# A conditioned feed-forward layer and a generated adapter: ternary weights made over two steps, the generator's base summed on GpSimd, and the low halves of the activations made later

## The chip, the core and the metric

The kernel runs on one core of one Trainium2 chip. Its engines are TensorE (PE, matmuls), VectorE (DVE), ScalarE (ACT), GpSimd (POOL) and SyncE (SP, which here only issues DMAs). The metric is the device time of one execution in microseconds (us), taken as the median of several executions.

## The reference, cut to what matters

There are 32 sequences of 256 rows with 256 columns. Layer 0 is a feed-forward layer with a scaled norm, a gate, and a product in which activations and weights are quantized; layer 1 is an adapter whose weight matrices are generated for each sequence from its condition vector.

```python
# layer 0
scale = cond @ norm_w.T + 1.0
ms = jnp.mean(x * x, axis=-1, keepdims=True)
h = x * (scale[:, None, :] * jax.lax.rsqrt(ms + EPS))
u = h @ up_w.T                       # (rows, 2048)
val, gate = jnp.split(u, 2, axis=-1)
h = val * jax.nn.gelu(gate, approximate=False)
y = act_quant(h) @ weight_quant(down_w).T    # ternary weights: -1, 0, 1 over a scale
x = y + x
# layer 1
dWd = ((h_lang @ Wdd.T + bdd) * DELTA_SCALE).reshape(B, BN, D)
dWu = ((h_lang @ Wdu.T + bdu) * DELTA_SCALE).reshape(B, D, BN)
down = jax.nn.relu(jnp.einsum('bld,bnd->bln', x, Wd + dWd) + bd)
up = jnp.einsum('bln,bdn->bld', down, Wu + dWu) + bu
return x + up
```

## The kernel before

The rows are cut into 64 tiles of 128 (two to a sequence), and every engine runs a loop over steps `s` = 0, 1, 2, ...; step `s` holds the feed-forward work of tile `s` and, beside it, work of other tiles at fixed lags. Each engine's instructions are written out in program order and run in that order; engines meet at semaphores. There is no scheduler.

A product in nearly full precision is made of three matmuls of 16-bit parts: high by high, high by low, low by high. So most operands are split: `xs_hi` and `xs_lo` (scaled activations, `scaled_high` on ACT, `scaled_low` on DVE), `up_hi` and `up_lo` (up weights), `wsplit` (generator weights; `high_part` on ACT, `low_part` partly on DVE, L578, and partly on POOL as four instructions, L364).

In step `s` TensorE does, in this order: `up(s, 0)` (12 matmuls of 512 columns into `u_val[0]` and `u_gate[0]`), `down(s - 3)` (8 matmuls), `up(s, 1)` (12 matmuls), and then either `generate(s - 2)` (48 small matmuls, in steps 2 to 17), or the adapter's `middle` and `output`. `up(s, c)` overwrites the banks that tile `s - 1` left, so it waits until `gate(s - 1, c)` on DVE (L642, signalled as `hid_done`) has read them. `generate(q)` waits for both low parts of chunk `q`; its second half also waits for `evacuate(q - 1, 0)` on DVE (L588, signalled as `gen_done`), because the generator has three banks. `gelu(s, c)` on ACT (L471) reads `u_gate[c]` and needs the norm factor `rms` of the sequence, which POOL makes in `rsqrt(b)`: eleven small instructions in a row, L375 to L386.

`ternary()` on DVE makes the ternary down weights once, in step 1: a scale (L604, L607) and three passes over 2048 columns (L609, L612, L615). `base_sum()` on DVE adds the generator's bias to the static adapter weights, once, in step 2 (L597, L600). `scaled_low(b)` stands in step `2b - 1`, ahead of the residual (L716) and of the two evacuations of that step; TensorE asks for it in step `2b`:

```python
if s % TPB == 0:
    pe.wait_ge(xs_done, s // TPB + 1)
up(s, 0)
```

Before its first real work TensorE runs matmuls on a tile of ones, whose result nobody reads (`idle(IDLE_FIRST)`, `idle(IDLE_SECOND)`, L798).

SP's queue issues every large load in program order: activations (`load_x`), up and down weights, generator chunks (`load_chunk`, 1 MB each), and the transposes of the quantized tiles.

Of the kernel before, what the change touches and what calls it, by code (L numbers as in the profile page):

```python
# [16 lines left out]
ALU = mybir.AluOpType  # L17
# [4 lines left out]
B, S, D = 32, 256, 256  # L22
# [3 lines left out]
TPB = S // P  # L26
# [42 lines left out]


IDLE_FIRST = 8
IDLE_SECOND = 12


LAST_T = NT - 1
# [49 lines left out]
def build(nc, xT, xn, condT, norm_wT, up_wT, down_wT, WdT, bd, WuT, bu, WddT, bddT, WduT, bduT, out):  # L125
    with ExitStack() as ctx:
# [146 lines left out]
        def _(sp):  # L273
# [49 lines left out]
                sp.dma_start(bias_raw[:, i, :], b).then_inc(ld_small, 16)  # L323
            sp.dma_start(bd_col[:], bd).then_inc(ld_small, 16)
            sp.dma_start(bu_row[:], bu.to_broadcast([P, D])).then_inc(ld_small, 16)
            load_chunk(1)
            for s in range(END):
                if s <= NT:
                    for t in split_tiles(s - 1):
                        transpose_x1(t)  # L330
                if 0 <= s - 1 < NT:
                    transpose_q(s - 1)
                if s >= NT:
                    for t in split_tiles(s):
                        transpose_x1(t)
                for b in sequences(s, -2):
                    if b < LAST_B:
                        store(b)
                    else:
                        store_last()  # L340
                if s % TPB == 0 and s // TPB + 2 < B:
                    load_x(s // TPB + 2)
                for q in chunk(s, -2):
                    if q >= 2:
                        load_chunk(q)
# [6 lines left out]
        def _(pool):  # L352
# [50 lines left out]
            def output_bias(b):  # L403
# [4 lines left out]
                for i in range(TPB):  # L408
                    nc.gpsimd.tensor_tensor(out_s[:, b % OUT_SLOTS, i], x1[:, (b * TPB + i) % X1_SLOTS], bu_row[:], ALU.add  # L409
                                            ).then_inc(outb_done, 1)  # L410

            def middle_low(b):
                pool.wait_ge(relu_done, b * 2 + 2)
                nc.gpsimd.tensor_tensor(mid_lo[:], mid[:], mid_hi[:], ALU.subtract).then_inc(mid_done, 1)  # L414

            rsqrt(0)
            for s in range(END):
                for b in sequences(s, -1):
                    if b < LAST_B:
                        middle_low(b)  # L420
                if 0 <= s - 2 < NT:
                    dequantization(s - 2)
                for b in sequences(s, 0):
                    output_bias(b)
                if s == 1:
                    rsqrt(1)
                for q in chunk(s, 0):
                    low_part(q)
                for b in scales(s):
                    if b > 1:  # L430
                        rsqrt(b)
                for b in sequences(s, 2):
                    adapter_low(b)
# [123 lines left out]
        def _(dve):  # L557
# [24 lines left out]
            def evacuate(q, n):  # L582
                w = q // NGC
                at = (q % NGC * 2 + n) * 2 * BCH
                if q == 0:
                    dve.wait_ge(base_ready, 2)
                dve.wait_ge(gen_full, 2 * q + n + 1)
                nc.vector.scalar_tensor_tensor(  # L588
                    out=adapt[:, w, :, at:at + 2 * BCH].rearrange("p b m -> p m b"),
                    in0=gen_ps[(2 * q + n) % 3][:].rearrange("p (m b) -> p m b", b=B),  # L590
                    scalar=DELTA_SCALE * A_SCALE / (W_SCALE * C_SCALE),
                    in1=base[:, w, at:at + 2 * BCH].unsqueeze(2).to_broadcast([P, 2 * BCH, B]),
                    op0=ALU.mult, op1=ALU.add).then_inc(gen_done, 1)

            def base_sum():
                dve.wait_ge(ld_small, 16 * N_SMALL)
                nc.vector.scalar_tensor_tensor(out=base[:], in0=bias_raw[:], scalar=DELTA_SCALE, in1=base[:],  # L597
                                               op0=ALU.mult, op1=ALU.add).then_inc(base_ready, 1)
                dve.wait_ge(base_ready, 1)
                nc.vector.tensor_scalar(base[:], base[:], A_SCALE, None, ALU.mult).then_inc(base_ready, 1)  # L600

            def ternary():
                dve.wait_ge(absum_full, 1)
                nc.vector.tensor_scalar(wsum[:, 1:2], sum_ps, 1.0 / (D * FF), QUANT_EPS, ALU.mult, ALU.max  # L604
                                        ).then_inc(tern_ready, 1)
                dve.wait_ge(tern_ready, 1)
                nc.vector.reciprocal(wsum[:, 2:3], wsum[:, 1:2]).then_inc(tern_ready, 1)  # L607
                dve.wait_ge(tern_ready, 2)
                nc.vector.tensor_scalar(raw_down, raw_down, wsum[:, 2:3], ROUND, ALU.mult, ALU.add  # L609
                                        ).then_inc(tern_ready, 1)  # L610
                dve.wait_ge(tern_ready, 3)
                nc.vector.tensor_scalar(raw_down, raw_down, ROUND + 1.0, ROUND - 1.0, ALU.min, ALU.max  # L612
                                        ).then_inc(tern_ready, 1)
                dve.wait_ge(tern_ready, 4)
                nc.vector.tensor_scalar(tern[:].rearrange("p j d -> p (j d)"), raw_down, ROUND, None,  # L615
                                        ALU.subtract).then_inc(tern_ready, 1)
# [127 lines left out]
            for n in range(NC * KD):  # L744
# [3 lines left out]
                                               in1=up_part(up_hi, c, k), op0=ALU.mult, op1=ALU.subtract  # L748
                                               ).then_inc(up_ready, 1)
            for s in range(END):  # L750
                if s < NT:
                    gate(s, 0)
                if s % TPB == 1 and s // TPB + 1 < B:
                    scaled_low(s // TPB + 1)
                if s == 1:
                    rsqrt_guess(1)
                    ternary()
                if s == 2:
                    base_sum()
                if 0 <= s - DOWN < NT:  # L760
                    residual(s - DOWN)
                if s < NT:
# [2 lines left out]
                for q in chunk(s, 2):  # L765
                    evacuate(q, 0)
                    evacuate(q, 1)
                for b in scales(s):
                    if b > 1:
                        rsqrt_guess(b)  # L770
# [24 lines left out]
        def _(pe):  # L795
# [16 lines left out]
            def up(t, c):  # L812
# [2 lines left out]
                after(pe, hid_done, (t - 1) * NC + c + 1)  # L815
                cols = slice(t % TPB * P, (t % TPB + 1) * P)
                for k in range(KD):
                    passes = ((xs_hi, up_hi), (xs_hi, up_lo), (xs_lo, up_hi))
                    for n, (a, w) in enumerate(passes):
                        if t == 0 and n == 0:  # L820
                            pe.wait_ge(up_hi_ready, c * KD + k + 1)
                        if t == 0 and n == 1:
                            pe.wait_ge(up_ready, c * KD + k + 1)
                        for v, dst in enumerate((u_val[c], u_gate[c])):
                            ins = nc.tensor.matmul(dst[:], a[:, t // TPB % 2, k, cols], w[:, c, k, v, :],  # L825
                                                   start=(k == 0 and n == 0), stop=(k == KD - 1 and n == 2))
# [74 lines left out]
            for s in range(END):  # L901
                if s < NT:
                    if s % TPB == 0:
                        pe.wait_ge(xs_done, s // TPB + 1)
                    up(s, 0)
                if s == 1:

# [55 lines left out]
```

## Time and profile before

| what | value |
|---|---|
| median of 3 runs | 492.7 us (492.66 to 493.88) |
| the profiled execution's own time | 491.39 us |
| its span | 489.6 us |
| TensorE busy | 469.5 us, 96% |
| VectorE busy | 387.7 us, 79% |
| ScalarE busy | 364.7 us, 74% |
| GpSimd busy | 265.4 us, 54% |

The span runs from the first to the last instruction of the profiled execution; 1.8 us of its own time lie around it. Busy time is the share of the span in which an engine had an instruction under way. TensorE's is close to the whole, so the interest is in the few stretches in which it was not busy, and in the stretches in which its clock was not the full one.

### The profile page before, as it was taken

The numbers are of one execution on the slowest core, as the hardware profiler recorded it, in microseconds if no ns is written. First come the engines' busy times: TensorE is split into PE (matmuls) and PEld (weight loads), VectorE is DVE, ScalarE is ACT, GpSimd is POOL, SyncE is SP. The second block draws the span as 40 slices with busy tenths as digits, with TensorE's granted clock in tenths as the row PEclk, the third lists the DMA queues.
The fourth block names the chain that finished last, engine by engine and source line by source line (L and its number), as shares of the span: only waits on it lengthen the run. The fifth ranks groups of instructions, "written<-read, shape, count | busy, mean of one in ns | idle before, by whom it ended". The sixth has DMA issues, their size and how long they took to land.

```text
span 489.6 us, 9974 instructions
## 1 busy us (share of the span) xinstructions
PE 469.5 (96%) x3252; PEld 271.2 (55%) x3252; DVE 387.7 (79%) x778; ACT 364.7 (74%) x631; POOL 265.4 (54%) x680
## 2 busy tenths in 40 slices
PE   8969999999999999999999999999999999999955
PEld 8435555555555555555555555555555555555533
DVE  3798988998898887878778787877778777777683
ACT  4888999899896777777686768677777777667551
POOL 3277565675654557556565665665444444444452
PEclk9989999999999999999999999999999999999986
DMA  7958867587763575656645566664455544553443
GB/s 247 352 94 208 257 166 227 164 221 226 185 173 44 117 121 120 158 122 139 144 84 141 131 162 130 122 154 95 115 119 143 126 110 108 129 131 75 88 96 107
DMA packets 120547, 71.65 MB, mean 146 GB/s; under 512 B 104688, under 2 KB 105648, under 8 KB 118320
## 3 DMA queue, kind: packets, MB, share of 16 engines
q1 hardware_dynamic: 120336, 70.94, 58.6%
q8 instruction: 26, 0.43, 0.4%
q14 instruction: 25, 0.20, 0.2%
q10 hardware_dynamic: 160, 0.07, 0.1%
HBM read 37.44 MB, written 8.39 MB: 94 GB/s over the span
## 4 chain that ended last, share of the span: by engine, by line
PE 77%; DVE 6%; ACT 5%; issue 5%; POOL 3%; DMA 2%; SPq 1%; ACTq 0%; DVEq 0%; POOLq 0%
PE bank L825 57%; PE bank L835 10%; PE bank L873 4%; PE bank L863 4%; DVE xs_lo L621 2%; DMA xn_s<-in_xn 2%; PE bank L849 2%; ACT stage L441 2%; ACT wsplit L446 2%; DVE adapt L588 1%; ACT gel L471 1%; POOL wsplit L364 1%; DVE x L716 1%; ACT xs_hi L454 1%; POOL ad_lo L400 1%
## 5 line engine op out<-in xcount | busy, mean ns | idle before, releaser
L642 DVE SCALAR_TENSOR_TENSOR hid<-bank,rms,gel 128x512 f32<-128x512 f32 x128 | 95.8, 748 | 75.7 <-ACT gel L471 72.4
L825 PE MATMUL bank<-up_hi,xs_hi 128*128 128x512 f16 x512 | 153.1, 381 | 2.7 <-DVE hid L642 2.4
L825 PE MATMUL bank<-up_lo,xs_hi 128*128 128x512 f16 x512 | 152.8, 380 | 0.5 <-DVE up_lo L747 0.5
L471 ACT ACTIVATE gel<-bank,rms 128x512 f32<-128x512 f32 x128 | 87.6, 684 | 88.2 <-PE bank L825 87.1
L825 PE MATMUL bank<-up_hi,xs_lo 128*128 128x512 f16 x512 | 152.8, 380 | 0.0
L825 PEld LDWEIGHTS bank<-up_lo,xs_hi 128*128 128x128 f16 x512 | 50.1, 98 | 61.9 <-DVE up_lo L747 1.9
L825 PEld LDWEIGHTS bank<-up_hi,xs_lo 128*128 128x128 f16 x512 | 50.2, 98 | 60.7 <-issue 0.6
L650 DVE TENSOR_REDUCE amax<-hid 128x1 f32<-128x1024 f32 x63 | 76.9, 1220 | 2.2
L364 POOL TENSOR_TENSOR wsplit<-stage,wsplit 128x288 f16<-128x288 f32 x64 | 56.4, 911 | 38.5 <-ACT wsplit L446 38.5
L477 ACT ACTIVATE hid<-hid,amax 128x1024 f32<-128x1024 f32 x64 | 72.4, 1132 | 1.5 <-DVE amax L676 1.2
L835 PE MATMUL bank<-tern,qT 128*128 128x256 bf16 x512 | 67.2, 275 | 4.6 <-DMA qT<-qn 3.2
L825 PEld LDWEIGHTS bank<-up_hi,xs_hi 128*128 128x128 f16 x512 | 48.8, 98 | 37.7 <-issue 3.6
L400 POOL TENSOR_TENSOR ad_lo<-adapt,ad_hi 128x256 f16<-128x256 f32 x64 | 44.1, 709 | 46.2 <-DVE ad_hi L733 46.2
L486 ACT ACTIVATE qn<-hid 128x1024 bf16<-128x1024 f32 x64 | 67.1, 1048 | 0.5
L375 POOL TENSOR_TENSOR nwt<-nwt 128x2 f32<-128x2 f32 x96 | 23.4, 243 | 77.8 <-DVE nwt L635 72.8
L835 PEld LDWEIGHTS bank<-tern,qT 128*128 128x128 bf16 x512 | 50.2, 98 | 24.2 <-DMA qT<-qn 3.5
L409 POOL TENSOR_TENSOR out_s<-x,bu_row 128x256 f32<-128x256 f32 x64 | 49.5, 794 | 0.0
L414 POOL TENSOR_TENSOR mid_lo<-mid,mid_hi 128x256 f16<-128x256 f32 x31 | 21.9, 705 | 33.5 <-ACT mid_hi L510 33.5
L723 DVE TENSOR_TENSOR x1n<-x,x1n 128x256 f16<-128x256 f32 x64 | 37.8, 607 | 0.1
L621 DVE SCALAR_TENSOR_TENSOR xs_lo<-xT_s,scaleT,xs_hi 128x256 f16<-128x256 f32 x64 | 34.5, 578 | 0.2 <-ACT xs_hi L454 0.2
L493 ACT CAST x1n<-x 128x256 f16<-128x256 f32 x63 | 24.0, 399 | 12.9 <-DVE x L716 12.9
L716 DVE SCALAR_TENSOR_TENSOR x<-bank,amax,xn_s 128x256 f32<-128x256 f32 x64 | 30.4, 474 | 2.9 <-PE bank L835 2.9
(89 smaller groups left out, 625.3 us busy)
## 6 DMA issues: line engine op xcount, KB each, us to landing
xT_s<-in_xT SPq DMA_DIRECT2D x32, 256.0 KB, 3.4
xn_s<-in_xn SPq DMA_DIRECT2D x32, 256.0 KB, 3.7
stage<-in_WddT SPq DMA_DIRECT2D x8, 1024.0 KB, 5.7
stage<-in_WduT SPq DMA_DIRECT2D x8, 1024.0 KB, 5.2
out<-out_s SPq DMA_DIRECT2D x31, 256.0 KB, 2.3
adapt<-in_up_wT SPq DMA_DIRECT2D x4, 512.0 KB, 7.5
x<-in_down_wT SPq DMA_DIRECT2D x1, 1024.0 KB, 11.5
qT<-qn SPq DMA_TRANSPOSE x64, 3.1
```

Source lines behind the costliest of these rows:

```text
L364: ins = nc.gpsimd.tensor_tensor(wsplit[:, q % 2, 1, cols], stage[:, q % 2, cols], wsplit[:, q % 2, 0, cols], ALU.subtract)
L400: ins = nc.gpsimd.tensor_tensor(lo, src, hi, ALU.subtract)
L409: nc.gpsimd.tensor_tensor(out_s[:, b % OUT_SLOTS, i], x1[:, (b * TPB + i) % X1_SLOTS], bu_row[:], ALU.add).then_inc(outb_done, 1)
L471: nc.scalar.activation(gel[:, c], u_gate[c][:], ACT.Gelu, scale=rms[:, t // TPB % XN_SLOTS, t % TPB:t % TPB + 1]).then_inc(gelu_done, 1)
L477: nc.scalar.activation(part, part, ACT.Copy, bias=ROUND, scale=amax[:, t % AM_SLOTS, 2:3]).then_inc(q_done, 1)
L486: nc.scalar.activation(qn[:, t % 2, cols], hid[:, t % 2, cols], ACT.Copy, bias=-ROUND).then_inc(qn_done, 1)
L621: ins = nc.vector.scalar_tensor_tensor(out=xs_lo[:, b % 2, k], in0=xT_s[:, b % XT_SLOTS, k], scalar=scaleT[:, k, b:b + 1], in1=xs_hi[:, b ...
L642: nc.vector.scalar_tensor_tensor(out=hid[:, t % 2, c * 512:(c + 1) * 512], in0=u_val[c][:], scalar=rms[:, t // TPB % XN_SLOTS, t % TPB:t % ...
L650: nc.vector.tensor_reduce(a[:, 0:1], hid[:, t % 2], AX.X, ALU.max, apply_absolute_value=True).then_inc(amax_done, 1)
L723: nc.vector.tensor_tensor(parts[:, 1], x1[:, t % X1_SLOTS], parts[:, 0], ALU.subtract).then_inc(x1_lo_done, 1)
L825: ins = nc.tensor.matmul(dst[:], a[:, t // TPB % 2, k, cols], w[:, c, k, v, :], start=(k == 0 and n == 0), stop=(k == KD - 1 and n == 2))
L835: ins = nc.tensor.matmul(y_ps[:, 0:D], qT[:, t % QT_SLOTS, f], tern[:, f], start=(f == 0), stop=(f == JF - 1))
```

## The change

The three passes of the ternary weights are no longer in a row: the first stays in step 1, the second stands at the start of step 2, ahead of `gate(2, 0)`, and the third behind that gate. The base sum moves from DVE to POOL, where it takes three instructions in place of two (multiply, add, multiply) and stands in step 2 between `dequantization(0)` and `low_part(1)`. Twelve idle matmuls become nine. From the third sequence on, `scaled_low` stands behind the residual and the two evacuations of its step; TensorE then starts `up(s, 0)` of an even step on `xs_hi` alone and waits for `xs_lo` at the third matmul, for which the passes change their order. `load_x(2)` is issued ahead of `load_chunk(1)`.

```diff
-IDLE_SECOND = 12
+IDLE_SECOND = 9
...
             sp.dma_start(bu_row[:], bu.to_broadcast([P, D])).then_inc(ld_small, 16)
+            load_x(2)
             load_chunk(1)
...
-                if s % TPB == 0 and s // TPB + 2 < B:
+                if s % TPB == 0 and 2 < s // TPB + 2 < B:
                     load_x(s // TPB + 2)
...
+            def base_sum():
+                pool.wait_ge(ld_small, 16 * N_SMALL)
+                nc.gpsimd.tensor_scalar(bias_raw[:], bias_raw[:], DELTA_SCALE, None, ALU.mult).then_inc(base_ready, 1)
+                pool.wait_ge(base_ready, 1)
+                nc.gpsimd.tensor_tensor(base[:], base[:], bias_raw[:], ALU.add).then_inc(base_ready, 1)
+                pool.wait_ge(base_ready, 2)
+                nc.gpsimd.tensor_scalar(base[:], base[:], A_SCALE, None, ALU.mult).then_inc(base_ready, 1)
...
+                if s == 2:
+                    base_sum()
                 for q in chunk(s, 0):
                     low_part(q)
...
-                    dve.wait_ge(base_ready, 2)
+                    dve.wait_ge(base_ready, 3)
...
-            def ternary():
+            def ternary_first():
...
+            def ternary_second():
                 dve.wait_ge(tern_ready, 3)
...
+            def ternary_third():
                 dve.wait_ge(tern_ready, 4)
...
             for s in range(END):
+                if s == 2:
+                    ternary_second()
                 if s < NT:
                     gate(s, 0)
-                if s % TPB == 1 and s // TPB + 1 < B:
-                    scaled_low(s // TPB + 1)
                 if s == 1:
+                    scaled_low(1)
                     rsqrt_guess(1)
-                    ternary()
+                    ternary_first()
                 if s == 2:
-                    base_sum()
+                    ternary_third()
...
                     evacuate(q, 1)
+                if s % TPB == 1 and 1 < s // TPB + 1 < B:
+                    scaled_low(s // TPB + 1)
...
-                    passes = ((xs_hi, up_hi), (xs_hi, up_lo), (xs_lo, up_hi))
+                    passes = ((xs_hi, up_hi), (xs_lo, up_hi), (xs_hi, up_lo))
                     for n, (a, w) in enumerate(passes):
+                        if t % TPB == 0 and c == 0 and k == 0 and a is xs_lo:
+                            pe.wait_ge(xs_done, t // TPB + 1)
                         if t == 0 and n == 0:
                             pe.wait_ge(up_hi_ready, c * KD + k + 1)
-                        if t == 0 and n == 1:
+                        if t == 0 and n == 2:
                             pe.wait_ge(up_ready, c * KD + k + 1)
...
-                        pe.wait_ge(xs_done, s // TPB + 1)
+                        pe.wait_ge(xs_hi_done, (s // TPB + 1) * KD)
```

First, DVE's program from the first ternary pass in step 1 to the first gate of step 2, in the kernel before; the 2048-column rows are the ternary passes, `hid` is a gate, `wsplit` the low part of generator chunk 0.

```order
L609 TENSOR_SCALAR x<-x,wsum 128x2048
L612 TENSOR_SCALAR x<-x 128x2048
L615 TENSOR_SCALAR tern<-x 128x2048
L642 SCALAR_TENSOR_TENSOR hid<-bank,rms,gel 128x512
L650 TENSOR_REDUCE amax<-hid 128x1
L653 TENSOR_SCALAR amax<-amax 128x1
L656 RECIPROCAL amax<-amax 128x1
L578 SCALAR_TENSOR_TENSOR wsplit<-stage,wsplit 128x896
L642 SCALAR_TENSOR_TENSOR hid<-bank,rms,gel 128x512
L597 SCALAR_TENSOR_TENSOR base<-bias_raw,base 128x512
L600 TENSOR_SCALAR base<-base 128x512
```

The same place in the changed kernel:

```order
L613 TENSOR_SCALAR x<-x,wsum 128x2048
L650 SCALAR_TENSOR_TENSOR hid<-bank,rms,gel 128x512
L658 TENSOR_REDUCE amax<-hid 128x1
L661 TENSOR_SCALAR amax<-amax 128x1
L664 RECIPROCAL amax<-amax 128x1
L589 SCALAR_TENSOR_TENSOR wsplit<-stage,wsplit 128x896
L618 TENSOR_SCALAR x<-x 128x2048
L650 SCALAR_TENSOR_TENSOR hid<-bank,rms,gel 128x512
L623 TENSOR_SCALAR tern<-x 128x2048
```

Two passes have moved behind the low part of chunk 0, one on each side of the first gate of step 2, and the base sum is gone from here.

Second, POOL's program from the end of `rsqrt(1)` to the start of `rsqrt(2)`: `rms` is the last of the small instructions, each `wsplit` row a low part of four instructions. Before:

```order
L386 TENSOR_TENSOR rms<-nwt 128x2
L364 TENSOR_TENSOR wsplit<-stage,wsplit 128x288 x4
L393 TENSOR_TENSOR amax<-amax,wsum 128x1
L364 TENSOR_TENSOR wsplit<-stage,wsplit 128x288 x4
L375 TENSOR_TENSOR nwt<-nwt 128x2
```

Changed:

```order
L387 TENSOR_TENSOR rms<-nwt 128x2
L365 TENSOR_TENSOR wsplit<-stage,wsplit 128x288 x4
L394 TENSOR_TENSOR amax<-amax,wsum 128x1
L415 TENSOR_SCALAR bias_raw<-bias_raw 128x512
L417 TENSOR_TENSOR base<-base,bias_raw 128x512
L419 TENSOR_SCALAR base<-base 128x512
L365 TENSOR_TENSOR wsplit<-stage,wsplit 128x288 x4
L376 TENSOR_TENSOR nwt<-nwt 128x2
```

The three base instructions stand ahead of the low part of chunk 1, and behind that of chunk 0.

Third, DVE in an odd step of the generator's stage (step 3), from its first to its second gate. Before:

```order
L642 SCALAR_TENSOR_TENSOR hid<-bank,rms,gel 128x512
L621 SCALAR_TENSOR_TENSOR xs_lo<-xT_s,scaleT,xs_hi 128x256 x2
L716 SCALAR_TENSOR_TENSOR x<-bank,amax,xn_s 128x256
L588 SCALAR_TENSOR_TENSOR adapt<-bank,base 128x16x32 x2
L642 SCALAR_TENSOR_TENSOR hid<-bank,rms,gel 128x512
```

Changed:

```order
L650 SCALAR_TENSOR_TENSOR hid<-bank,rms,gel 128x512
L724 SCALAR_TENSOR_TENSOR x<-bank,amax,xn_s 128x256
L599 SCALAR_TENSOR_TENSOR adapt<-bank,base 128x16x32 x2
L629 SCALAR_TENSOR_TENSOR xs_lo<-xT_s,scaleT,xs_hi 128x256 x2
L650 SCALAR_TENSOR_TENSOR hid<-bank,rms,gel 128x512
```

The two `xs_lo` instructions have changed places with the residual and the two evacuations; the second gate stands where it stood.

## Rows read from the trace of the kernel before

**Rows 1.** Stretches: us, then each engine's busy us (instructions), TensorE's granted clock, DMA.

```profile
42.46:58.11 15.65, 15.13 (x167) 9.04 (x164) 14.04 (x25) 14.75 (x22) 9.38 (x22) 1.00 0.82 192
152.00:460.00 308.00, 308.00 (x1784) 173.06 (x1781) 241.20 (x528) 222.72 (x421) 163.97 (x457) 1.00 0.54 122
```

**Rows 2.** Waits, whole span: us in total, times, longest.

```profile
PE bank L849 <- DVE adapt L588: 4.1, 7, 0.7
```

**Rows 3.** Timeline, one odd step: start, us, instruction; DVE first, then PE and POOL.

```profile
54.47 1.53 DVE L621 SCALAR_TENSOR_TENSOR xs_lo<-xT_s,scaleT,xs_hi 128x256 f16<-128x256 f32 x2
55.92 0.47 DVE L716 SCALAR_TENSOR_TENSOR x<-bank,amax,xn_s 128x256 f32<-128x256 f32 x1
56.31 1.94 DVE L588 SCALAR_TENSOR_TENSOR adapt<-bank,base 128x512 f32<-128x512 f32 x2
58.10 0.72 DVE L642 SCALAR_TENSOR_TENSOR hid<-bank,rms,gel 128x512 f32<-128x512 f32 x1
...
55.80 0.38 PE L825 MATMUL bank<-up_hi,xs_lo 128*128 128x512 f16 x1
58.11 0.60 PE L825 MATMUL bank<-up_hi,xs_hi 128*128 128x512 f16 x2
65.56 0.60 PE L825 MATMUL bank<-up_hi,xs_hi 128*128 128x512 f16 x2
...
59.98 3.66 POOL L364 TENSOR_TENSOR wsplit<-stage,wsplit 128x288 f16<-128x288 f32 x4 [0.78 <-ACT wsplit L446]
```

**Rows 4.** Timeline, 20 to 35 us: DVE, POOL, ACT, PE.

```profile
23.23 1.29 DVE L609 TENSOR_SCALAR x<-x,wsum 128x2048 f32<-128x2048 f32 x1
26.96 0.75 DVE L642 SCALAR_TENSOR_TENSOR hid<-bank,rms,gel 128x512 f32<-128x512 f32 x1
29.26 1.65 DVE L578 SCALAR_TENSOR_TENSOR wsplit<-stage,wsplit 128x896 f16<-128x896 f32 x1
...
23.29 1.28 POOL L377 TENSOR_TENSOR nwt<-nwt 128x2 f32<-128x2 f32 x1
24.65 1.18 POOL L379 TENSOR_TENSOR nwt<-nwt,threehalf 128x2 f32<-128x2 f32 x1
27.17 0.19 POOL L375 TENSOR_TENSOR nwt<-nwt 128x2 f32<-128x2 f32 x1
29.08 0.19 POOL L386 TENSOR_TENSOR rms<-nwt 128x2 f32<-128x2 f32 x1
29.23 4.10 POOL L364 TENSOR_TENSOR wsplit<-stage,wsplit 128x288 f16<-128x288 f32 x4
...
29.31 0.69 ACT L471 ACTIVATE gel<-bank,rms 128x512 f32<-128x512 f32 x1 [0.86 <-POOL rms L386]
...
27.85 1.01 PE L825 MATMUL bank<-up_hi,xs_hi 128*128 128x512 f16 x2 [2.44 <-DVE hid L642]
34.87 0.59 PE L825 MATMUL bank<-up_hi,xs_hi 128*128 128x512 f16 x2
```

**Rows 5.** Instructions of the low part on POOL, 28 to 60 us: ns min/median/max.

```profile
L364 POOL TENSOR_TENSOR wsplit<-stage,wsplit x17: 726/732/1584, 29.2 to 60.0; 128x288 f16<-128x288 f32 x17
```

**Rows 6.** Stretches behind TensorE's two longest gaps; columns as in rows 1.

```profile
27.80:31.10 3.30, 3.25 (x8) 1.16 (x9) 3.23 (x5) 2.40 (x7) 2.91 (x8) 0.50 0.01 1
477.00:479.00 2.00, 1.78 (x9) 1.26 (x10) 0.00 (x0) 0.00 (x0) 1.50 (x3) 0.50 0.45 99
```

**Rows 7.** Timeline, start of the program: the idle matmuls; GpSimd's first tensor instruction.

```profile
5.93 5.18 PE L798 MATMUL bank<-ones 128*128 128x128 f32 x24
...
8.55 0.19 POOL L375 TENSOR_TENSOR nwt<-nwt 128x2 f32<-128x2 f32 x1 [7.38 <-DVE nwt L635]
```

**Rows 8.** An odd step behind the generator: DVE's timeline, one row of the chain.

```profile
203.70 0.87 DVE L621 SCALAR_TENSOR_TENSOR xs_lo<-xT_s,scaleT,xs_hi 128x256 f16<-128x256 f32 x2
204.89 0.68 DVE L739 SCALAR_TENSOR_TENSOR out_s<-bank,out_s 128x512 f32<-128x512 f32 x1
...
206.34 2.59 PE bank L825 x12
```

More of the change, by code:

```diff
@@ L593, in evacuate @@
                     op0=ALU.mult, op1=ALU.add).then_inc(gen_done, 1)
[L595 to L600, printed above, removed]
-            def ternary():
+            def ternary_first():
                 dve.wait_ge(absum_full, 1)
```

## The prediction, made before the changed kernel ran

> **What bounds the kernel now.** I read the stretches first. From 152 to 460 us TensorE is busy for 308.00 of 308.00 us at the full clock, while DVE has 241 and ACT 223 [rows 1]. Nothing done for the other engines there can shorten that stretch, and what is gained ahead of 152 us reaches the end. So three places remain: the generator's stage (steps 2 to 17), the start, and the tail behind 460 us, which the change doesn't touch.
>
> In the generator's stage two steps take 15.65 us [rows 1]. The waits name one thing there: the generator's matmuls wait for an evacuation, 4.1 us in 7 waits [rows 2]. The timeline of such an odd step shows why. TensorE's last pair of up matmuls starts at 55.80 us (0.22 us into the pair) and the next tile's first at 58.11; DVE ran its gate, then `xs_lo` from 54.47, and only then the residual and two evacuations, from 55.92 to 58.10 [rows 3]. An up matmul of 512 columns takes 0.22 us, so `up` ended at 56.02 and `generate` took 2.09 us. Without the wait it would be about 1.41: of the next step's 7.45 us (58.11 to 65.56 [rows 3]), 24 up matmuls at 0.216 and 8 half as long leave 1.40. The gap is 0.68 us each time, in 7 odd steps.
>
> At the start, TensorE waits 2.44 us for the gate that stands behind the three ternary passes, and restarts at 27.85 us at half the clock for 3.3 us [rows 4, 6]. But then comes `generate(0)`, which needs POOL's low part of chunk 0. POOL ends that at 33.33 us, and the next `up` starts at 34.87 [rows 4]. So POOL sets the start: whatever TensorE does sooner ahead of 33.3 us is worth nothing by itself. POOL's chain is `rsqrt(1)`, then four L364 instructions.
>
> **The lock between DVE and POOL.** A small POOL instruction takes 0.19 us and 0.27 from start to start (27.17 to 29.08 for seven), but one took 1.28 beside the pass L609, and ended as that did [rows 4]; the next, 1.18, beside the second pass. The low part takes 0.73 us for a piece alone (0.69 from start to start) and up to 1.58 [rows 5]: with L578 started at the same moment it took 4.10 for four [rows 4]. So the two engines take turns, instruction by instruction, at something they share, and POOL's end is its own work plus DVE's instructions of that kind in between. The Trainium skill's GPSIMD Engine Reference (section 8, Key points) says that GpSimd shares SBUF interfaces with VectorE instructions in a two-port mode or with two SBUF inputs; by that rule the passes moved into step 2 slow the low part too, as the sum below has it.
>
> **The change, part by part.**
>
> *Ternary split, start.* DVE is free at 24.55 us (L609 from 23.23 plus its time) instead of 26.96; `gate(1, 1)` moves there, 2.4 us sooner, and the low part L578 from 29.26 to 26.85. POOL's `rsqrt(1)` is stretched once and not three times: its instruction of 27.17 comes at 24.65 + 2 x 0.27 = 25.19, so `rms` is ready at 27.3, 2.0 sooner. So far POOL gains 2.0. Then the turns: L578 holds until 27.9 (1.0); four pieces at 0.69 make 2.8; and both moved passes now lie between these pieces, since `gel(2, 0)`, freed by `rms` at 27.3, lets the first gate of step 2 run at once: 2 x 1.23 = 2.5. 27.9 + 2.8 + 2.5 = 33.1, against 33.33. The gain at `generate(0)` is 0.25 us; bounds are 0 and 2.5 (passes behind POOL's pieces).
>
> *The clock.* `up(2, 1)` was the work in which TensorE waited; now it ends early. `up(2, 0)` starts some 0.5 us sooner and ends at 24.8, the gate is done at 25.3, `up(2, 1)` runs to 27.9 at the full clock. Then TensorE has nothing until 33.1: 5.2 us idle, twice the gap behind which the half clock was seen. It restarts with `generate(0)`, and that time is on the path. Half clock lasted 3.3 us behind the first gap, and at least from 477 to 479 behind the one in the tail [rows 6]. Half of it is lost: 1.6 us; I take 1.7, with 0.7 (the clock back within `generate(0)`) and 2.5 (half as long again as the first time) as bounds. Before, the same loss lay under the wait for POOL. The Trainium skill, TensorE: Matmul & The Clock Gate (section The HAM clock gate), says the half clock is the default and activity releases it; it speaks against moving a gap to a place with no cover.
>
> *Base sum on POOL.* It leaves 2.0 us of DVE's step 2, which nobody waited for. On POOL the nearest row is L364: 0.69 us for 288 columns, so 1.23 for 512 and 3.7 for three; below, three small ones, 0.6. The low part of chunk 1 would end at 33.4 + 3.7 + 2.8 + 1.0 (one turn of DVE) = 40.9. TensorE asks at 33.1 + 1.4 + 6.05 + 1.7 = 42.3. Hidden with 1.4 us to spare; with a full clock TensorE would ask at 40.6 and wait 0.3. Cost 0.
>
> *Idle matmuls.* Three of twelve (24 records, 5.18 us [rows 7]) are 1.3 us. The first up matmul comes up to 0.7 us sooner; all that lies ahead of POOL's 33.1. Gain 0. If TensorE's clock fell for want of them, it would show in the first 20 us. `load_x(2)` ahead of `load_chunk(1)`, and the order of the passes: 0 for the same reason; ACT asks for chunk 1 only behind `gel(2, 1)`, after 31 us.
>
> *Low halves behind the evacuations.* In an odd step DVE's gate ends at 54.47, 4.5 us behind the start of `up(5, 0)` (58.11 - 2.09 - 6.05 = 49.97, with 6.05 for two `up` and a `down`). The residual and two evacuations take 2.2, `xs_lo` 0.87 without POOL's pieces beside it [rows 8]; that is 7.55, and 8.2 if it takes 1.53 as now. The evacuation is there 0.8 us before TensorE's second half asks for it, so the 0.68 goes. TensorE wants `xs_lo` two matmuls into the next step: 7.45 + 0.43 = 7.9. It is in time by 0.3, or 0.3 late. A second limit stands close: POOL's low part ended at 59.98 + 3.66 = 63.64 [rows 3], 7.62 behind the end of `up(5, 1)`, and its chain (gelu, ACT's three passes, POOL) doesn't get shorter. TensorE now reaches that generator after 1.41 + 6.05 = 7.46. It waits 0.16. So each pair gains 0.5: 7 x 0.5 = 3.5. Bounds: 1.8 (`xs_lo` late) and 4.8 (no new wait). ACT has 14.75 us busy in a pair [rows 1] that would take 15.1; it isn't the limit yet.
>
> *Behind the generator.* `xs_lo` moves behind the residual and the total (0.4 and 0.6), so it ends at 205.5 where it ended at 204.5; `up` of the next step starts at 206.34 [rows 8]. Cost 0.
>
> **The sum** against the execution of 491.39 us: -0.25 + 1.7 - 3.5 = -2.05, so 489.3. The median of the runs lies 1.3 above that execution, so 490.6 is the time I expect.
>
> **The rivals.**
>
> *No price for the clock.* The pieces of POOL slip in ahead of the passes, so that the idle time is short, or the clock is back within a microsecond; and no wait of 0.16 appears. Then -0.25 - 4.8 = -5.0, up to -6 with an earlier `generate(0)`: 487.4. For it: the margin at the second limit is a tenth of a microsecond. Against it: 2.44 us of idling was enough for the half clock.
>
> *`xs_lo` is the new wait.* It comes behind the evacuations at 8.2, TensorE waits 0.3 to 0.4 in each even step, and the pairs give 1.8: -0.25 + 1.7 - 1.8 = -0.35, 492.3, no change. For it: 1.53 us was its time in this stage. Against it: POOL's pieces had ended at 55.7, ahead of its new place.
>
> *Slower: GpSimd's new kind of instruction.* POOL has run no tensor-scalar instruction so far. The base sum may take T = 3.7 and no more than 1.4 more is covered; beyond T = 5.1 `generate(1)` waits, and the kernel gets slower than before beyond 5.1 + 2.05 = 7.2. At T = 9.7 it is 490.6 + 4.6 = 495.2. For it: three instructions in a row in front of a low part that TensorE waits for. Against it: the first tensor instruction of POOL ran in 0.19 us, at once [rows 7]. The Trainium skill's GPSIMD Engine Reference (section 2.1) gives about 6 us for the first call of a freshly loaded kernel, with nothing visible in a profile; by that rule T would be 9.7, but rows 7 show no such delay.
>
> **How the numbers follow.** A difference under 0.3% (1.5 us) can't be told from none here. Chances: the forecast 45% (own range 489.2 to 491.9), no price for the clock 23%, late `xs_lo` 24%, slower 8%. The forecast and the first rival are faster but for the upper part of the forecast's range, above 491.2: faster 0.60. The late `xs_lo` and that upper part: same 0.31. Slower 0.09, with the tail's clock, which can come out either way by 1 us, in it. The range takes in both neighbours and their bounds: 487.2 to 493.0.
>
> **What would show it.** Right: 7 waits of the generator for `adapt` gone; `generate(0)` at 33 us with TensorE's clock at one half behind it; pairs of 15.1 us from 42 to 150 us; a small wait for POOL's low part in even steps. Wrong: the low part of chunk 0 ends well ahead of 33 us; a wait of TensorE for `xs_lo`; a base instruction of over 2 us; ACT busy without a gap from 42 to 150 us.

## The result, and the profile after

| | before | after |
|---|---|---|
| median of the runs, us | 492.68 (4 runs, 491.78 to 493.88) | 486.5 (4 runs, 485.69 to 487.76) |
| profiled execution: own time, span | 491.39, 489.6 | 486.9, 485.1 |
| start of `up(4, 0)` and of `up(18, 0)` in the chain | 42.62, 152.52 | 43.93, 148.84 |

The ratio is 0.9875, with a 95% interval from 0.9844 to 0.9906: 1.3% faster, where 0.4% was forecast, and 0.7 us below the range's lower end. The two profiled executions lie 4.5 us apart, the medians 6.2.

Waits of the changed kernel, whole span: us in total, times, longest. The waits for `adapt` [rows 2] are gone, and one long wait for POOL's low part stands ahead of `generate(0)`.

```profile
PE bank L862 <- POOL wsplit L365: 4.8, 1, 4.8
...
PE bank L838 <- DVE hid L650: 1.5, 1, 1.5
```

The start, from the timeline of the changed kernel: start, us, instruction (compare [rows 4]).

```profile
24.57 0.75 DVE L650 SCALAR_TENSOR_TENSOR hid<-bank,rms,gel 128x512 f32<-128x512 f32 x1
24.79 0.20 POOL L380 TENSOR_TENSOR nwt<-nwt,threehalf 128x2 f32<-128x2 f32 x1
26.88 1.07 DVE L589 SCALAR_TENSOR_TENSOR wsplit<-stage,wsplit 128x896 f16<-128x896 f32 x1
26.99 1.02 POOL L380 TENSOR_TENSOR nwt<-nwt,threehalf 128x2 f32<-128x2 f32 x1
27.87 1.22 DVE L618 TENSOR_SCALAR x<-x 128x2048 f32<-128x2048 f32 x1
28.08 1.05 POOL L387 TENSOR_TENSOR rms<-nwt 128x2 f32<-128x2 f32 x1
29.10 3.78 POOL L365 TENSOR_TENSOR wsplit<-stage,wsplit 128x288 f16<-128x288 f32 x4
30.56 1.72 DVE L623 TENSOR_SCALAR tern<-x 128x2048 bf16<-128x2048 f32 x1
33.02 0.21 PE L862 MATMUL bank<-cdiag_hi,wsplit 128*128 128x64 f16 x1 [4.80 <-POOL wsplit L365]
33.10 1.50 POOL L415 TENSOR_SCALAR bias_raw<-bias_raw 128x512 f32<-128x512 f32 x1
```

The second gate comes 2.4 us sooner, as forecast. Then two small POOL instructions each hold for a DVE instruction (26.99 beside L589, 28.08 beside the pass L618), and the low part holds for the last pass. TensorE waits 4.8 us and then runs at the half clock. In stretches of the changed kernel (columns as in rows 1; the granted clock is the number after POOL's) that reads:

```profile
29.00:30.00 1.00, 0.00 (x0) 0.00 (x0) 0.19 (x2) 0.83 (x2) 1.00 (x3) 1.00 0.00 0
31.00:32.00 1.00, 0.00 (x0) 0.00 (x0) 1.00 (x1) 1.00 (x2) 1.00 (x2) 0.50 0.00 0
35.00:36.00 1.00, 1.00 (x16) 0.72 (x14) 0.93 (x4) 1.00 (x3) 0.95 (x1) 0.50 0.89 352
37.00:38.00 1.00, 1.00 (x6) 0.39 (x4) 0.00 (x0) 0.00 (x0) 1.00 (x1) 0.95 1.01 273
58.70:73.70 15.00, 14.99 (x164) 8.93 (x161) 13.40 (x25) 14.12 (x21) 9.76 (x24) 1.00 0.80 212
```

The last of them is a pair of steps in the generator's stage: TensorE is busy in 14.99 of 15.00 us. The chain of the same kernel shows the price of the half clock, and what is left of waits in that stage: start, us, what.

```profile
33.02 2.72 PE bank L862 x48
35.74 3.33 PE bank L838 x12
...
42.53 1.40 PE bank L862 x48
43.93 2.59 PE bank L838 x12
...
64.89 1.56 PE bank L862 x48
...
148.84 2.59 PE bank L838 x12
...
463.99 0.02 issue
```

`generate(0)` takes 2.72 us where later ones take 1.40, and the next `up` 3.33 where they take 2.59: 2.06 us in all. Of the seven even steps from 4 to 16, three have a longer `generate` (1.56 us at 64.89, and 1.55 twice) and four have 1.40; the odd step 17 has 1.49.

The account from the two chains: +1.31 us at `up(4, 0)`; -4.99 from there to `up(18, 0)` (109.90 us before, 104.91 after); -0.15 to the end of the last `up` (467.82 and 463.99), and -0.67 behind it, in the tail. The sum is -4.5.

The tail's 0.67 can be read from one row of each kernel: the eight `down` matmuls behind TensorE's last long wait. Before, the granted clock was 0.50 when they started; in the changed kernel it was 1.00 until 474.0 us and fell near their end.

```profile
477.22 1.89 PE L835 MATMUL bank<-tern,qT 128*128 128x256 bf16 x8 [3.24 <-DMA qT<-qn]
```
```profile
473.32 1.26 PE L848 MATMUL bank<-tern,qT 128*128 128x256 bf16 x8 [3.19 <-DMA qT<-qn]
```

It is chance and no effect of the change: in `e5_after`, the same kernel, they took 1.89 us again.

### The profile page after: what moved, and what is told of

It is laid out like the page before. It is cut to its first block, busy times and chain, and to the rows that moved or that the text cites. A ratio compares the mean times of both kernels' runs of the same rounds, so it can differ in the third digit from the quotient of the medians.

```text
span 485.1 us, 9963 instructions
## 1 busy us (share of the span) xinstructions
PE 467.1 (96%) x3246; PEld 270.3 (56%) x3246; DVE 384.2 (79%) x776; ACT 365.0 (75%) x631; POOL 267.8 (55%) x683
## 4 chain that ended last, share of the span: by engine, by line
PE 90%; POOL 4%; DVE 2%; issue 2%; ACT 1%; POOLq 0%; DVEq 0%; ACTq 0%
PE bank L838 65%; PE bank L848 11%; PE bank L862 5%; PE bank L886 4%; PE bank L876 4%; PE bank L809 1%; POOL wsplit L365 1%; POOL nwt L378 1%; POOL nwt L380 1%; POOL ad_lo L401 1%; DVE hid L650 0%; POOL nwt L376 0%; POOL nwt L383 0%; DVE xs_lo L629 0%; ACT gel L482 0%
## 5 line engine op out<-in xcount | busy, mean ns | idle before, releaser
L365 POOL TENSOR_TENSOR wsplit<-stage,wsplit 128x288 f16<-128x288 f32 x64 | 53.0, 856 | 33.2 <-ACT wsplit L457 33.2
L599 DVE SCALAR_TENSOR_TENSOR adapt<-bank,base 128x512 f32<-128x512 f32 x32 | 31.2, 1054 | 0.0
```

The source lines that it names most:

```text
L365: ins = nc.gpsimd.tensor_tensor(wsplit[:, q % 2, 1, cols], stage[:, q % 2, cols], wsplit[:, q % 2, 0, cols], ALU.subtract)
```

## The experiments

Ratios are to the kernel before on the same chip, with a 95% interval. Three groups of four ran together, beside 17, 11 and 23 runs of the kernel before, whose medians were 491.23, 492.37 and 491.69 us.

**First group: which part gives, which costs.** `e1_xs_only` is the kernel before with only the low halves moved and asked for later.

```diff
-                if s % TPB == 1 and s // TPB + 1 < B:
-                    scaled_low(s // TPB + 1)
                 if s == 1:
+                    scaled_low(1)
...
                     evacuate(q, 1)
+                if s % TPB == 1 and 1 < s // TPB + 1 < B:
+                    scaled_low(s // TPB + 1)
...
-                        pe.wait_ge(xs_done, s // TPB + 1)
+                        pe.wait_ge(xs_hi_done, (s // TPB + 1) * KD)
```

> The kernel before with one part of the change: scaled_low behind the evacuations, TensorE asking for it at the third matmul. Theory A (the generator's stage gives the whole gain; the start costs some): the seven waits for the evacuation go, 0.68 to 0.71 us each, and nothing is lost at the start, so 4.9 us faster than before, about 487.8, and faster by about 1 us than it would be with the start's parts. Theory B (both parts gave some): 3 us or less, 489.5 or more.

Measured: 486.63 us, 0.9903 [0.9881, 0.9924]. The waits for `adapt` are gone with this edit alone, and it gives 4.6 us. The whole change gives 6.2 us in the result and 5.0 in its repeat `e5_after`, and the intervals overlap, so nothing shows that the other edits add to it. Its start is the order of before, and yet TensorE's clock fell at another place. Its chain and stretches:

```profile
33.93 2.72 PE bank L852 x48
...
44.47 2.59 PE bank L828 x12
```
```profile
28.00:31.00 3.00, 2.65 (x12) 0.97 (x10) 2.93 (x6) 1.78 (x4) 2.65 (x7) 1.00 0.00 0
33.90:37.20 3.30, 3.27 (x50) 2.85 (x51) 3.20 (x5) 2.60 (x4) 1.47 (x3) 0.50 0.72 194
```

In the profile of before the half clock stood from 27.8 to 31.1 us [rows 6], under the wait for POOL. Here that stretch ran at 1.00, and the clock fell behind the second gap, on the path: `up(4, 0)` starts 1.85 us later than in the profile of before. Of that, 0.46 is a later `generate(0)` (33.93 against 33.47, since POOL's pieces took 4.50 us and not 4.10); 1.4 is the clock. The second gap was 3.3 us here and 1.3 there, because `up(2, 1)` ran ahead of it at the full clock. With before's start, too, the loss can be on the path. The Trainium skill's TensorE: Matmul & The Clock Gate (Part 1) says that how much of a kernel runs at the low clock varies between runs of the same kernel; these two traces, whose first gaps are 2.44 and 2.59 us, are in keeping with it, though the kernels differ in the place of `xs_lo`.

`e2_start_only` is the changed kernel with the low halves' place and asking undone (the diff of `e1_xs_only` the other way).

> The changed kernel with scaled_low and TensorE's asking as before: only the start's parts (ternary split, base sum on GpSimd, nine idle matmuls, load_x(2) first). Theory A: generate(0) starts 0.3 us sooner but at half the clock, up of step 4 comes 1.3 us later than before, so 1.3 us slower than before, about 494. Theory B (the start gains): 1 to 2 us faster than before.

Measured: 492.27 us, 1.0018 [1.0005, 1.0032]: the start's edits alone cost 1.0 us. The seven waits for `adapt` are back (4.2 us), and the chain has `generate(0)` at 33.28 with 2.72 us and `up(4, 0)` at 44.87.

`e3_warm` is the changed kernel with ten idle matmuls ahead of `generate(0)`.

```diff
+                if s == 2:
+                    idle(10)
                 for q in chunk(s, 1):
                     generate(q)
```

> The changed kernel with ten idle matmuls (0.42 us each, 4.2 us) ahead of generate(0), in the gap from 28.2 to 33.0 us. Theory A (half the clock on the path costs 1.7 us): generate(0) takes 1.4 us in place of 2.7, the first up matmuls 0.22 in place of 0.43, 1.7 to 2.0 us faster than the changed kernel, 484.7. Rival (what is lost to the clock is given back by a wait for GpSimd's low part of chunk 1 or for DVE): under 0.5 us.

Measured: 486.29 us, 0.9897 [0.9877, 0.9916], which can't be told from the changed kernel's 0.9875 to 0.9898. They filled only half of the gap. Timeline of `e3_warm`:

```profile
28.18 2.39 PE L809 MATMUL bank<-ones 128*128 128x128 f32 x20
33.16 0.21 PE L862 MATMUL bank<-cdiag_hi,wsplit 128*128 128x64 f16 x1 [2.58 <-POOL wsplit L365]
```

I had sized them by the 0.216 us a record of [rows 7]; here one took 0.12. The clock still fell, and `generate(0)` took 2.72 us. This run decides nothing on the clock's price.

`e4_tern_late` runs the second and third pass behind the second gate of step 2, behind POOL's pieces.

```diff
-                if s == 2:
-                    ternary_second()
                 if s < NT:
                     gate(s, 0)
...
-                if s == 2:
-                    ternary_third()
...
+                if s == 2:
+                    ternary_second()
+                    ternary_third()
                 for t in split_tiles(s):
```

> The changed kernel with the second and third ternary pass behind quant_scale(2), so neither lies among GpSimd's pieces of chunk 0. Theory A (DVE and GpSimd take turns instruction by instruction): rms(1) is ready 1 us sooner, the low part of chunk 0 ends near 31.0 in place of 32.9, generate(0) starts 1.9 us sooner; the passes now meet the base sum, so generate(1) comes at about 41.1 in place of 42.5: 1.2 us faster than the changed kernel. Rival (GpSimd's pieces are slow by themselves here, no turns): low part of chunk 0 ends as now, no change.

Measured: 484.8 us, 0.9867 [0.9844, 0.989]. Timeline of POOL, and the chain:

```profile
27.78 0.19 POOL L387 TENSOR_TENSOR rms<-nwt 128x2 f32<-128x2 f32 x1
27.92 2.80 POOL L365 TENSOR_TENSOR wsplit<-stage,wsplit 128x288 f16<-128x288 f32 x4
```
```profile
30.87 2.12 PE bank L861 x48
32.99 3.66 PE bank L837 x12
...
41.85 2.59 PE bank L837 x12
```

Without the passes beside them, the same four POOL instructions took 2.80 us and not 3.78, and `rms` 0.19 and not 1.05. `generate(0)` came 2.15 us sooner and `up(4, 0)` 2.08. So in the traces the passes' turns cost the changed kernel some 2 us, and the place into which the ternary work was moved is not the best one. The medians show less of it: the intervals of the two kernels overlap, and the ratio is 0.4 to 1.5 us below the changed kernel's two.

**Second group: the clock, and the later asking.** `e5_after` is the changed kernel again, without an edit, as a measure of how far it repeats.

> The changed kernel once more, on the chip of the runs sent with it. If the parts add up (the late low halves alone 0.9903 of before, the start's parts alone 1.0018), it comes at 0.992 of before, 3.8 us faster; if the start's parts help beside the late low halves, at 0.9875 or lower. It is also the mark for the other runs here.

Measured: 487.41 us, 0.9898 [0.9877, 0.992]. `generate(0)` at 32.93, `up(4, 0)` at 44.0: the same execution as in the first profile to 0.1 us. The gain over before is 5.0 us here and was 6.2 in the result, so two medians of one kernel differ by about 1 us against before. It lies between the two expectations and decides for neither.

`e6_warm19` has 19 idle matmuls in the gap, enough to fill it at 0.12 us a record.

```diff
+                if s == 2:
+                    idle(19)
                 for q in chunk(s, 1):
                     generate(q)
```

> The changed kernel with nineteen idle matmuls ahead of generate(0). Ten took only 2.4 us, left 2.6 us idle, and the clock fell all the same; nineteen take 4.5 us and fill the gap up to 33.0 us. Theory A (half the clock on the path costs 1.7 us): the granted clock stays at 1.00, generate(0) takes 1.4 us, up of step 3 2.6 us, 1.5 to 1.9 us faster than the changed kernel. Rival (given back to a wait): under 0.5 us.

Measured: 485.65 us, 0.9869 [0.9852, 0.9886]. Timeline, one stretch, and the waits from 20 to 160 us:

```profile
27.61 4.41 PE L809 MATMUL bank<-ones 128*128 128x128 f32 x38
32.59 0.19 PE L862 MATMUL bank<-cdiag_hi,wsplit 128*128 128x64 f16 x1 [0.57 <-POOL wsplit L365]
```
```profile
33.00:34.00 1.00, 1.00 (x41) 1.00 (x38) 0.97 (x2) 1.00 (x3) 1.00 (x1) 1.00 0.89 123
```
```profile
PE bank L862 <- POOL wsplit L365: 1.1, 2, 0.6
```

The clock stayed at 1.00, and `up(18, 0)` starts 1.7 us sooner than in `e5_after` (147.05 and 148.76 in the timelines); the median is 1.8 lower. So the half clock did lie on the changed kernel's path, and 1.7 was its price in the forecast. Part of it is masked: with the full clock, `generate(1)` waits 0.54 us for POOL's low part, which now stands behind the base sum. The forecast had 0.3 for that.

`e7_ask_early` is the changed kernel with `xs_lo` asked for ahead of the step, as before.

```diff
-                        pe.wait_ge(xs_hi_done, (s // TPB + 1) * KD)
+                        pe.wait_ge(xs_done, s // TPB + 1)
```

> The changed kernel with TensorE's order of passes and its wait for xs_lo as before (at the first matmul of an even step), the low halves still behind the evacuations. xs_lo ended within 0.1 us of the start of up in the even steps; with it, the later asking hides what is late. Theory A: 0.05 to 0.2 us in each of 7 even steps, 0.3 to 1.5 us slower than the changed kernel. Rival (the low halves are always in time): no change.

Measured: 488.16 us, 0.9919 [0.9903, 0.9935]. `up(18, 0)` starts at 149.91, 1.15 us later than in `e5_after`. Of that, 0.22 stands already at `up(4, 0)`; the other 0.9 is a small wait in the even steps. The place in DVE's order gives most of the gain, the later asking the rest. The medians alone (488.16 and 487.41, intervals that overlap) would not show it.

`e8_late_base_warm` puts the passes behind the second gate as `e4_tern_late` does, the base sum behind them on DVE, and 12 idle matmuls ahead of `generate(0)`.

```diff
+                if s == 2:
+                    ternary_second()
+                    ternary_third()
+                    base_sum()
                 for t in split_tiles(s):
```

> A kernel from the findings: ternary passes two and three and the base sum (on DVE again) behind quant_scale(2), and twelve idle matmuls ahead of generate(0). Theory A: generate(0) starts at 30.9 us at the full clock, generate(1) waits for nothing: 2.0 (start) + 1.7 (clock) = 3.5 to 3.9 us faster than the changed kernel, about 1.7 to 2 us faster than with the late passes alone. Rival (something behind it sets the start, such as chunk 1 on ACT and GpSimd): no faster than with the late passes alone.

Measured: 486.81 us, 0.9888 [0.987, 0.9906]: no gain over the changed kernel. `generate(0)` came at 31.40 and at the full clock, but what stood behind it was then late. Waits from 20 to 160 us:

```profile
PE bank L845 <- DVE tern L620: 1.6, 1, 1.6
...
PE bank L859 <- DVE adapt L589: 1.1, 1, 1.1
```

**Third group: where before's time went, and a better version.** `e9_before_warm` is the kernel before with idle matmuls in both gaps of its start.

```diff
+                if s == 2:
+                    idle(9)
                 if s < NT:
                     up(s, 1)
...
+                if s == 2:
+                    idle(12)
                 for q in chunk(s, 1):
                     generate(q)
```

> The kernel before with nine idle matmuls ahead of up(2, 1) and twelve ahead of generate(0). Question: was the loss to the half clock in most executions of the kernel before too (in its start as seen in the run with the late low halves alone, which fell to half the clock at 33.9 us) and merely not in the one profiled. Theory A: yes, 0.8 to 1.7 us faster than before. Theory B (only the changed kernel pays, as the prediction had it): no change.

Measured: 490.89 us, 0.9983 [0.9972, 0.9993]. The clock was 1.00 through the start, and nothing else in the program moved: in its profiled execution `up(4, 0)` starts at 42.65, in that of before at 42.62. So over the executions of before the median cost of the clock on the path is 0.8 us (0.3 to 1.4), though in the profiled one it cost nothing there.

`e10_xs_early` is the changed kernel with `xs_lo` back ahead of the residual and the evacuations, but still asked for late.

```diff
+                if s % TPB == 1 and s // TPB + 1 < B:
+                    scaled_low(s // TPB + 1)
                 if s == 1:
-                    scaled_low(1)
...
-                if s % TPB == 1 and 1 < s // TPB + 1 < B:
-                    scaled_low(s // TPB + 1)
```

> The changed kernel with scaled_low at its old place, ahead of the residual and the evacuations; TensorE asks for it late as in the changed kernel. Theory A (the place is what counts): the seven waits for the evacuation are back, 4.8 to 5 us slower than the changed kernel, 492. Rival (the late asking gives a good part): 490 or less.

Measured: 491.85 us, 1.0008 [0.9996, 1.0021]. The wait is back in full, and the whole gain is gone:

```profile
PE bank L861 <- DVE adapt L599: 4.1, 7, 0.7
```

`e11_base_dve` is the changed kernel with the base sum on DVE, behind the third pass.

```diff
                 if s == 2:
                     ternary_third()
+                    base_sum()
```

> The changed kernel with the base sum on DVE, as two instructions behind the third ternary pass. GpSimd's three took 5.1 us (one turn of DVE among them), hidden: its low part of chunk 1 ended at 41.0, 1.5 us ahead of generate(1) at 42.5. Theory A: no change (within 0.5 us). Rival: DVE's 0.9 us delays its gates, 1 us slower; or GpSimd's chain counted, 1 us faster.

Measured: 486.11 us, 0.9881 [0.9866, 0.9896], between the two results of the changed kernel. By itself the engine of the base sum is worth nothing that these runs tell apart.

`e12_best` puts base sum and passes on DVE between the two gates of step 2, behind POOL's four pieces (a wait on their semaphore), with 11 idle matmuls ahead of `generate(0)`.

```diff
+                if s == 2:
+                    dve.wait_ge(w_lo_p, 1)
+                    base_sum()
+                    ternary_second()
+                    ternary_third()
                 if s < LAST_T:
                     gate(s, 1)
                     quant_scale(s)
```

> A kernel from the findings: behind the first gate of step 2 DVE waits for GpSimd's low part of chunk 0, then makes the base sum and the last two ternary passes, ahead of the second gate; eleven idle matmuls fill TensorE's gap. Theory A: generate(0) at 30.9 us at the full clock, down(0) waits at most 0.5 us for the ternary weights, generate(1) at 38.5 to 39.0 (42.5 in the changed kernel): 3 us faster than the changed kernel, 1.5 us faster than late passes alone. Rival (ACT's and DVE's chain to chunk 1 sets the start whatever is done): as late passes alone, 484.8.

Measured: 484.6 us, 0.9854 [0.984, 0.9868], the fastest of all: 1.5 us less than `e11_base_dve` beside it. Its timeline and its waits, whole span:

```profile
27.38 2.62 PE L807 MATMUL bank<-ones 128*128 128x128 f32 x22
30.50 0.19 PE L860 MATMUL bank<-cdiag_hi,wsplit 128*128 128x64 f16 x1 [0.50 <-POOL wsplit L365]
```
```profile
PE bank L860 <- DVE adapt L589: 1.0, 1, 1.0
...
PE bank L860 <- POOL wsplit L365: 0.5, 1, 0.5
```

`generate(0)` comes 2.5 us sooner than in the changed kernel, at the full clock. What is left is DVE: its first evacuation comes 1.0 us late. The ratio is 1.0 to 2.2 us below the changed kernel's two, where 3 was expected. `e4_tern_late` and this version overlap in their intervals.

## Why the prediction was right in direction and short in size

- **The ternary split.** Right: `generate(0)` at 33.02 (33.1 was said). The way there was another one: `rms` was ready at 29.1 and not at 27.3, since two turns with DVE fell on the last small instructions and not on the low part. The number of turns was the same, so that the time agrees to 0.1 us is in part luck. `e4_tern_late` shows the two passes' turns worth 2 us.
- **The clock.** Right that half clock stands behind the longer gap and on the path: +1.31 at `up(4, 0)` against -0.25 + 1.7 = +1.45. Of the 1.31, -0.45 is the earlier `generate(0)` (33.02 and 33.47) and +1.76 the rest: the 2.06 of the clock, less 0.3 of short waits that before had in its first two `generate` (1.56 and 1.53 us, where 1.40 is free). `e6_warm19` confirms it by taking it away. Incomplete: I read the price of before from one execution, in which the loss was covered. `e1_xs_only` and `e9_before_warm` show that before's executions pay it in part, 0.8 us. This is about half of the further 1.7 us by which the medians moved beyond the profiled pair. In the repeat, `e5_after`, the medians moved only 0.5 beyond it, so the other half may be no more than how far medians of four runs repeat; it stays open.
- **The failed step is "So each pair gains 0.5: 7 x 0.5 = 3.5".** The mechanism was right, the term was mis-sized: it measured 4.99, or 0.71 a pair. Four pieces make up the difference. A pair went from 15.65 us to 14.91 where TensorE never waits, so the gap was 0.74 and not 0.68 (0.4 over seven pairs); 15.65 less two free steps of 7.45 would have given 0.75 from the rows in hand. The last pair of before had waited 0.33 more: its `xs_lo` took 1.86 us and not 1.53. The new wait for POOL's low part came in three even steps of seven (0.15 to 0.16 each) and, with 0.09, in the odd step 17; it cost 0.54 us in all, not 7 x 0.16 = 1.12 (0.6 less). And 3.64 was rounded to 3.5.
- **The rest of the miss.** The median came 4.1 us under the forecast. The pairs make 1.5 of that, the tail 0.7, the start and the stage behind the generator 0.15 each. The last 1.7 is a second step that failed: "The median of the runs lies 1.3 above that execution" was carried over to the changed kernel, whose median lies 0.4 below its profiled execution. With 4.99 in the sum the forecast would have been 489.1, still 2.6 too high.
- **Why the new wait was smaller.** The forecast kept POOL's 3.66 us for the four pieces [rows 3] and said that this chain doesn't get shorter. It did. Timeline of the changed kernel: DVE and POOL in the odd step 5, in step 6, which has a wait, and in step 8, which has none:

```profile
53.19 1.07 DVE L589 SCALAR_TENSOR_TENSOR wsplit<-stage,wsplit 128x896 f16<-128x896 f32 x1
57.96 0.86 DVE L629 SCALAR_TENSOR_TENSOR xs_lo<-xT_s,scaleT,xs_hi 128x256 f16<-128x256 f32 x2
61.04 1.07 DVE L589 SCALAR_TENSOR_TENSOR wsplit<-stage,wsplit 128x896 f16<-128x896 f32 x1
75.94 1.07 DVE L589 SCALAR_TENSOR_TENSOR wsplit<-stage,wsplit 128x896 f16<-128x896 f32 x1
...
53.78 3.15 POOL L365 TENSOR_TENSOR wsplit<-stage,wsplit 128x288 f16<-128x288 f32 x4 [4.09 <-ACT wsplit L457]
61.23 3.56 POOL L365 TENSOR_TENSOR wsplit<-stage,wsplit 128x288 f16<-128x288 f32 x4 [0.56 <-ACT wsplit L457]
64.89 0.19 PE L862 MATMUL bank<-cdiag_hi,wsplit 128*128 128x64 f16 x1
76.30 3.38 POOL L365 TENSOR_TENSOR wsplit<-stage,wsplit 128x288 f16<-128x288 f32 x4 [1.01 <-ACT wsplit L457]
```

  DVE's L589 now starts ahead of POOL's pieces, and they lose only what is left of it when they start: 0.48 us of L589 is left at 53.78, 0.88 at 61.23 and 0.71 at 76.30, and the pieces take 3.15, 3.56 and 3.38 us, each time 2.67 or 2.68 more. In the even step of before, L578 started behind them (60.38, the pieces at 59.98 [rows 3]), and they took 3.66. That this order is the reason is argued from the rows; no run changed it alone. In step 6 the pieces end at 64.79 and TensorE starts at 64.89, 0.16 later than it could have; the waits view doesn't name so short a wait. `xs_lo` itself runs beside no piece of POOL and takes 0.86 us, as expected; it ends at 58.82, some 0.15 us behind the start of `up(6, 0)` and 0.3 ahead of the third matmul, which asks for it.
- **The tail.** I gave it 1 us either way inside the chances and 0 in the sum; it came out at -0.67 in the profiled pair, by the moment at which the clock fell.
- **Nothing, as said:** the base sum (1.50, 1.27 and 2.21 us; the low part behind it ended at 41.0, where 40.9 was said, and `generate(1)` asked at 42.5). The end agrees by luck: the three took 5.1 us from start to end and not 3.7, and the low part behind them met no turn of DVE (2.80 us, where 3.8 was said). Nothing came of the idle matmuls, `load_x(2)` and the stage behind the generator either, as far as the runs show: none of them changed one of these alone.
- **The rivals.** A late `xs_lo` didn't come; `e7_ask_early` shows that without the later asking it would have cost 0.9 us in this stage. The slow base sum didn't come: the last instruction, with 2.21 us, passed the 2 us that the forecast had named as a sign, but it lay beside DVE's L589 (35.38 to 36.90), and the three stayed hidden. The Trainium skill's GPSIMD Engine Reference (section 2.1) gives about 6 us for the first call of a freshly loaded kernel; the trace doesn't show it here: the first tensor-scalar instruction of GpSimd took 1.50 us. The rival without a price for the clock, 487.4 (its own terms give 487.6 to 486.7), lay nearest to the result. Its 4.8 us for the pairs was nearly right (4.99); the rest of its agreement is luck, since the price of the clock was there, and was there before in part too.

## What to carry to other kernels

When two short instructions stand in front of an evacuation for which TensorE waits, moving them behind it can pay the whole gap in every step, as it did here, if their reader can ask for them a few matmuls later; either edit alone gives less (`e7_ask_early`) or nothing (`e10_xs_early`). Ahead of the one thing that sets the start, keep DVE's long passes out of GpSimd's way: put them behind its last piece, not between its pieces. A gap of TensorE that sits on the path cost its length here and then the half clock behind it, and whether the kernel before paid that too can't be read from one profiled execution: fill the gap in both and compare.

## What the runs showed of the hardware

- The idle matmuls of 128x128 f32 took 0.216 us a record in the first 11 us of the program ([rows 7]), and 0.12 us in `e3_warm` (20 in 2.39 us) and `e6_warm19` (38 in 4.41 us). So they ran at about half the speed at the start, though the granted clock of that stretch reads 1.00; why is not shown. The `up` matmuls right behind them, from 10.95 us on, took their usual 0.22 us. A filler sized by its start-up time came out half as long as wanted.
- Ten idle matmuls that left 2.6 us of a 4.8 us gap open didn't keep the clock; 19 that left 0.57 us open did, and so did 11 in `e12_best` that left 0.50 open.
- On GpSimd a tensor-scalar instruction of 128x512 f32 took 1.50 us, more than a tensor-tensor of the same shape with its 1.27, though it reads one input only; one with a turn of DVE in it took 2.21. The three times are the same to 0.01 us in `e2_start_only`, `e3_warm`, `e5_after` and `e6_warm19`.
- DVE's and POOL's turns: the same `rms` instruction took 0.19 us in `e4_tern_late` and 1.05 beside a DVE pass of 1.22. The Trainium skill's GPSIMD Engine Reference (section 8, Key points) says that GpSimd shares its SBUF interfaces with VectorE and contends with DVE instructions in a two-port mode or with two SBUF inputs. The rows show the contention, though not the mode of the pass, and add that the small instruction ends only when the large one does (29.13 and 29.09).
